# Conditioned transformer block: the second norm's transpose moved from the even to the odd beats, the FFN's first product one beat sooner

## The reference

```
g, b   = t @ gw.T + gb, t @ bw.T + bb                  (one row per batch)
norm(x)= g * x * rsqrt(mean(x*x) + 1e-6) + b
x1     = x + softmax(q k' / sqrt(8)) v Wo              (q, k, v of norm1(x), 16 heads of width 8)
y      = (silu(norm2(x1) @ gate.T) * (norm2(x1) @ hid.T)) @ out.T     (hidden width 512)
result = x + (x1 + y)
```

## Time and profile before

| | |
|---|---|
| median of 3 runs | 251.71 us (250.55 to 251.79) |
| the profiled execution's own time | 252.26 us |
| its span | 250.4 us, so 1.86 us lie around it |
| mean granted TensorE clock | 0.993 of full speed |
| TensorE busy | 230.9 us |
| VectorE busy | 194.0 us |
| ScalarE busy | 156.7 us |
| GpSimd busy | 97.3 us |

### The profile page before, as it was taken

The page is one execution under the profiler, slowest core; times in us unless marked ns, Lnnn a source line. Parts: engine busy times, 40 slices in busy tenths (PEclk is TensorE's granted clock), DMA queues, the critical chain, the costliest instruction groups (busy, mean ns, idle before and its releaser), DMA issues.

```text
span 250.4 us, 8250 instructions
## 1 busy us (share of the span) xinstructions
PE 230.9 (92%) x3116; PEld 191.6 (77%) x3116; DVE 194.0 (77%) x473; ACT 156.7 (63%) x336; POOL 97.3 (39%) x169
## 2 busy tenths in 40 slices
PE   3579899899999999999999999999999999899894
PEld 2478676677778787878888787878787878687894
DVE  4648956668988998889888988898888888654673
ACT  5486565668766876687667766665566556656430
POOL 8654962454252625244524323242323232323320
PEclk9999889999999999999999999999999999999999
DMA  5872424001500060006000430034000000000001
GB/s 163 355 258 99 157 101 166 3 4 62 195 5 24 19 240 26 3 22 251 28 8 21 159 122 7 21 112 148 27 21 5 3 27 21 5 3 21 25 22 42
DMA packets 11203, 18.79 MB, mean 75 GB/s; under 512 B 1468, under 2 KB 4220, under 8 KB 11036
## 3 DMA queue, kind: packets, MB, share of 16 engines
q1 hardware_dynamic: 10780, 17.67, 19.5%
q10 hardware_dynamic: 384, 0.59, 0.7%
HBM read 3.22 MB, written 2.10 MB: 21 GB/s over the span
## 4 chain that ended last, share of the span: by engine, by line
PE 62%; issue 17%; DVE 8%; POOL 7%; ACT 3%; DMA 2%; SPq 0%; POOLq 0%; DVEq 0%; ACTq 0%
PE pv L500 10%; PE score L431 10%; PE proj L564 7%; PE aux L341 5%; PE aux L343 4%; PE aux L342 4%; DVE nmax L822 3%; PE aux L517 2%; PE aux L521 2%; DMA qs<-qp 2%; PE aux L572 2%; POOL inv L983 2%; PE proj L341 2%; PE pv L529 1%; PE aux L512 1%
## 5 line engine op out<-in xcount | busy, mean ns | idle before, releaser
L682 ACT ACTIVATE p_s<-score 128x1024 f32<-128x1024 f32 x64 | 65.7, 1026 | 34.0 <-PE score L431 33.9
L822 DVE TENSOR_REDUCE nmax<-raw 128x8 f32<-128x1024 f32 x60 | 73.1, 1219 | 5.0 <-PE score L413 2.7
L431 PEld LDWEIGHTS score<-qs,ks 32*128 32x128 f32 x512 | 34.1, 186 | 15.0 <-issue 11.5
L431 PE MATMUL score<-qs,ks 32*128 32x128 f32 x512 | 42.8, 284 | 2.7 <-DVE shift L832 1.9
L500 PE MATMUL pv<-p_s,va 128*32 128x128 f32 x1024 | 41.7, 281 | 0.2 <-ACT xn L700 0.2
L413 PE MATMUL raw<-ks,qs 31*128 31x128 f32 x480 | 40.2, 285 | 1.6 <-DMA qs<-qp 1.6
L881 DVE SCALAR_TENSOR_TENSOR gated<-th,aux 128x256 f32<-128x256 f32 x56 | 23.3, 416 | 18.7 <-ACT th L711 18.3
L341 PE MATMUL aux<-xn_hi,ffn_hi 128*128 128x256 f32 x112 | 36.5, 326 | 0.0
L996 POOL TENSOR_TENSOR xn_lo<-xn,xn_hi 128x128 fp32r<-128x128 f32 x32 | 14.7, 460 | 55.6 <-DVE xn_hi L872 55.6
L413 PEld LDWEIGHTS raw<-ks,qs 31*128 31x128 f32 x480 | 31.7, 186 | 1.8 <-DMA qs<-qp 1.8
L564 PE MATMUL proj<-ffn_out_s,hT 128*128 128x128 f32 x240 | 31.6, 275 | 0.0
(11 more groups left out here) (128 smaller groups left out, 431.6 us busy)
## 6 DMA issues: line engine op xcount, KB each, us to landing
ks<-kp SPq DMA_DIRECT2D x23, 256.0 KB, 2.7
qs<-qp SPq DMA_DIRECT2D x23, 256.0 KB, 2.6
out_y<-x_s SPq DMA_DIRECT2D x16, 128.0 KB, 1.8
x_s<-in_x SPq DMA_DIRECT2D x1, 1536.0 KB, 10.4
x_s<-in_x SPq DMA_DIRECT2D x2, 256.0 KB, 3.9
ffn_in_s<-in_ffn_in_w SPq DMA_DIRECT2D x1, 512.0 KB, 6.5
qs<-shift SPq DMA_DIRECT2D x30, 8.0 KB
attn_w_s<-in_attn_w SPq DMA_DIRECT2D x1, 256.0 KB, 5.7
```

The source lines that it names most:

```text
L431: return pe.matmul(score[:, pair_cols(e, j)], ks[buf(g)][tile_rows(e, t, TROWS), j, batch_cols(t)], qs[buf(g)][tile_rows(e, t, TROWS), j, ...
L682: act.activation(p_s[:, n % PBUF, :], score[:], ACT.Exp, scale=SCALE).then_inc(s_exp, 1)
L822: dve.tensor_reduce(heads[:, t % 2, :, :], raw_dst(g, t)[:].rearrange("l (e j m) -> l e j m", e=HALVES, j=HQ), AX.X, ALU.max, negate=True) ...
```

## The change

The four table numbers INV2, XT2, HI2 and FFN each become one smaller. With XT2 = 5 the transpose `d_xt2` falls in the odd beats, where `a_transpose` is, and it is issued directly behind that one and ahead of `d_out` and `c_wo`. HI2 = 6 puts `d_hi` and `d_lo` in the even beats, INV2 = 4 puts `d_inv` and `d_scale` there. FFN = 9 starts the FFN one beat sooner, so beat 9 loses its four unread products. `a_transpose` no longer waits for the second norm's activation of the beat before, and `d_xt2` no longer waits for the copy `c_ot` of the same beat. OUT, FINAL and RESID stay.

```diff
-    OT, TR2, NORM, TRO, WO, X1, INV2, XT2, HI2, RESID = 2, 2, 2, 3, 3, 4, 5, 6, 7, 6
-    FFN, OUT, FINAL, WSTEP = 10, 15, 17, HC + 1
+    OT, TR2, NORM, TRO, WO, X1, INV2, XT2, HI2, RESID = 2, 2, 2, 3, 3, 4, 4, 5, 6, 6
+    FFN, OUT, FINAL, WSTEP = 9, 15, 17, HC + 1
...
                 if T is not None:
                     if T == 1:
                         pe.wait_ge(s_shift0, MB)
-                    for f, i in due(T - 1, XT2, NB, 2):
-                        pe.wait_ge(s_xn2, NB * f + i + 1)
...
-            def d_xt2(g, i, T):
+            def d_xt2(g, i):
                 pe.wait_ge(s_xs2, NB * g + i + 1)
                 if g == G - 1 and i > 0:
                     pe.wait_ge(s_xn2, NB * g + i)
-                for f, n in due(T, OT, NB, 2):
-                    pe.wait_ge(s_ot, NB * f + n + 1)
                 pe.transpose(pv[:, 2 * L:3 * L], xs2[:, i, :], ident[:]).then_inc(s_xt2, 1)
...
                 for g, b in due(T, XT1, NB, 2, since=3):
                     a_transpose(g, b, T)
+                for g, i in due(T, XT2, NB, 2):
+                    d_xt2(g, i)
                 for w in range(WIN):
                     for g, half in due(T, OUT + WSTEP * w, 2):
                         d_out(g, w, half)
                 for g, i in due(T, WO, NB, 2):
                     c_wo(g, i)
-                for g, i in due(T, XT2, NB, 2):
-                    d_xt2(g, i, T)
```

## The result

The changed kernel took 256.44 us, the median of 4 runs (256.31 to 256.79). The kernel before, run beside it, took 251.75 us (4 runs, 250.55 to 253.17). The ratio is 1.0156, with a 95% interval of 1.0117 to 1.0196: slower, by 4.7 us. The forecast was 255.6 us. The profiled execution took 256.79 us with a span of 255.0.

What follows compares the result with a forecast made beforehand. TensorE was taken to bound most beats, VectorE's reduction start beats 2 and 6. Terms 2.9 + 0.9 + 0.5 - 0.5 + 0.1 = +3.9 us gave 255.6 us from the 251.71 median; range 251.4 to 257.4, likeliest case 254.5 to 256.8.

Steps and rivals of the forecast that it cites:

- What bounds: VectorE's start of reduction L822 sets the end of beats 2 and 6; TensorE's own work sets the other six.
- The held copy, 0.72 us four times: Beats 18, 26, 34, 42: moved d_hi copy waits for GpSimd's second subtraction, delaying the maxima 0.72 us each, 2.9 us.
- Not held: Rival: in beat 2 the copy gets in ahead of GpSimd's second subtraction; +0.9, 252.6 us; chance 0.19.
- Sharing: Rival: copy and GpSimd's subtraction both run at about half speed, 0.34 us a time; +2.0, 253.7 us; chance 0.10.
- Held twice: Rival: GpSimd's `d_inv` also gets in ahead of the copy, 5 x 0.62 more; 258.7 us; chance 0.07.
- the bound of 1.34: Upper bound in us per held copy in beat 2, if GpSimd's `d_inv` gets in ahead of it too.
- Faster, by the waits for `c_ot`: Rival: maxima have slack, so TensorE's 2.8 us of waits before transposes and 0.5 at the end go; 248.4 us; chance 0.10.
- Beat 6 and its like, 7 x 0.13 = 0.9: Beats 14, 22, 30, 38, 46, 54, 58: the copy delays the reduction by its issue distance, 0.13 us each.
- The low bound: Lower bound of the beat-6 term: 0.05 a beat as TensorE's slack hides part; sum 0.6 us.
- Beat 10, +0.5: Sooner FFN piece in beat 9 makes beat 10's maxima 0.8 us later, less 0.35 for removed waits; bounds -0.4 and +1.1.
- The end, -0.5: Last batch's norm: GpSimd does `inv` before `resid`, so `xs2` comes 0.5 us earlier; bounds -0.8 and 0.

Runs made afterwards that it cites:

- the early `a_hi`: Changed kernel with VectorE issuing the first norm's two copies (a_hi) ahead of the FFN's hidden product in beat 1; 251.03 us, ratio 0.9913.
- The reduction with one input: Kernel before plus one unread VectorE row-maximum reduction of x1 (128x128, SBUF) per batch, behind the squares' sum; 257.77 us, ratio 1.0234.
- The copy behind the maxima: Changed kernel with d_hi moved between the row maxima (b_max) and the shift (b_shift); 250.86 us, ratio 0.9958.
- the FFN a beat later: Changed kernel with FFN = 10 again, so that only the second norm's steps are moved; 256.96 us, ratio 1.0202.
- The added copies of that kernel: Kernel before plus one unread VectorE copy of x1 to a spare 128x128 tile per batch, behind the squares' sum; 263.54 us, ratio 1.0428.
- the kernel with the copy behind `c_norm`: Changed kernel with d_hi issued behind c_norm, no longer ahead of the row maxima, in all its beats; 258.35 us, ratio 1.0207.

## Why the prediction was right, step by step

- **What bounds.** Right: in the beats 2 and 6 VectorE's start of the reduction sets the end. When it moved by 0.67 the half grew by 0.66, when it moved by 0.13 the half grew by 0.14, and where the early `a_hi` took 1.08 away, 1.06 came back.
- **The held copy, 0.72 us four times.** The mechanism was right, the size a little too large: 0.67 us a time and 2.63 in all. The copy ended 0.08 us behind the subtraction, not 0.15 as in the pair of rows it was taken from, which was of a 128x256 copy (0.15 in all kernels; every held 128x128 copy ended 0.08 to 0.09 behind). The order on the two engines was right too: the squares' sum, held 0.23 us, gets in between the two subtractions, and the copy waits for the second. The Trainium skill's page "SBUF — State Buffer", section "SBUF: two separate sides", describes this as an exclusive lock on the port pair rather than a split of bandwidth, taken by two-port copies and by operations with two SBUF inputs. For GpSimd's subtraction and for `resid` all runs agree with it: beside one of them with 0.66 us left the copy takes 0.74 to 0.76 us, with 0.2 us left 0.28, and with none 0.21 to 0.23. The squares' sum with its two inputs takes 0.29 alone, and 0.31 to 0.58 beside a subtraction with 0.16 to 0.43 left, always ending 0.15 behind it. The reduction with one input takes 0.27 to 0.28 in all 32. For the power `inv` the traces differ from the page, and they decide: it didn't hold the copy. Where one came up in the kernel before with 0.39 us of `inv` left, it took its usual time:

```profile
237.59 0.22 DVE L872 CAST xn_hi<-xn 128x128 fp32r<-128x128 f32 x1
```

- **Not held** fell with the 0.74 us. **Sharing** fell with the length of the copy (0.43 us by half speed, 0.74 measured), with its end just behind GpSimd's instruction (0.08 to 0.09 us in two kernels), and with the reduction that was never slowed. **Held twice** fell: `inv` started at 112.31 and ran 0.54 us, but the copy was over at 112.43, with one hold. By the row just shown `inv` wouldn't have cost the 0.62 us of this rival even ahead of the copy; that price, and with it the bound of 1.34, took a hold by `inv` for granted.
- **Faster, by the waits for `c_ot`** fell as argued. These waits left, and the maxima's wait grew to 0.32 in beat 6. The copy behind the maxima, which removes the cost of the copy and keeps the waits' removal, left the period at 26.60.
- **Beat 6 and its like, 7 x 0.13 = 0.9.** Against the kernel before, four of the seven grew by 0.11 to 0.15 (beats 22, 30, 38, 46), as did 58; beats 14 and 54 didn't (-0.08, -0.02), nor did beat 50 (-0.03). So the sum was +0.56. Against the kernel with the copy behind the maxima, all seven are 0.12 to 0.16 longer, 0.98 in sum, so the copy's price was right. What the sum put at nothing is what left with the transposes and their waits: 0.23 us in beat 14 and 0.14 in beat 54 (that kernel against the kernel before), next to nothing in the steady beats. The low bound, written as 0.05 a beat and summed to 0.6, is 0.08 a beat (0.13 less 0.05).
- **Beat 10, +0.5** came out at +0.50, with the copy held there as well (the wait at L473 1.21 us). It was more than luck: with the FFN a beat later the stretch is 0.41 us shorter than before (the forecast credited 0.35 for the waits that left), and the sooner FFN, with the hold of the copy that comes with it, puts 0.91 on it (forecast 0.8).
- **The end, -0.5.** Only -0.17. This term was mis-sized, though its reason was right: `inv` does come first, and from the last addition of `x1` to the transpose it took 1.77 us (241.26 to 243.03) instead of 2.25 (236.26 to 238.51). But that addition itself came 0.23 later behind the last maxima's transpose, and the rest of the run was 0.08 longer. The rows of the end, against the earlier trace rows:

```profile
241.96 0.54 POOL L979 TENSOR_TENSOR inv<-ms,mhalf 128x1 f32<-128x1 f32 x1 [4.16 <-DVE ms L860]
...
243.03 0.33 PE L525 MATMUL pv<-ident,xs 128*128 128x128 f32 x1 [1.27 <-POOL xs L985]
```

- **What the sum left out.** The clock at the start: 1.08 us of the span's growth, and about as much of the medians' difference. By its steps the forecast was +3.9; the change is worth +2.9 to +3.3 at equal clock, and +3.5 by the table without its first row, so the steps are 0.4 to 1.0 too high. The medians are 4.7 apart because the runs of the changed kernel stood one level of the clock below those of the kernel before. That 255.6 came within 0.9 us of 256.44 is thus in part luck: the steps' excess and the clock's share that they left out have opposite signs.

Still open: why the granted clock differs between executions, why the power `inv` doesn't hold the copy, and whether ScalarE could write the second norm's rounded part (not tried).

## What to carry to other kernels

Before a copy or an operation with two SBUF inputs is moved on VectorE, look at what GpSimd runs at the new place: a copy of 0.22 us cost 0.67 beside a subtraction there, as part of a chain that TensorE waits for. Put it where VectorE waits anyway, but not behind its consumer's need: one place later than that cost 0.20 us a piece and 2 us at the end. And where a kernel's executions differ by a level of the clock, compare at equal clock before any story about 1 us is told.

## What was unexpected of the hardware

- The addition of `resid` (0.83 us on GpSimd) held the copy as the subtraction did: 0.75 us in both. The added copies of that kernel took 0.22 to 0.23 us in the beats 0 and 4 and 0.74 to 0.76 in the beats 2 and 6, none between.
- The power `inv` on GpSimd held no copy: 0.22 us for the copy with 0.39 us of it left. The hold can also go the other way: in the kernel with the copy behind `c_norm`, the copy at 241.15 came up 0.01 us behind the start of `xs2`'s scaling, took its 0.22, and the scaling took 0.49 us instead of 0.40.
- A `tensor_reduce` of one SBUF tile was held in none of 32 cases, beside the same subtraction that held the squares' sum of 0.29 us to 0.52.
- The granted clock of the first 40 us differs between executions of one kernel. The changed kernel took 253.8, 255.0 and 256.4 us at mean clocks of 1.000, 0.993 and 0.986, and the kernel before 250.5, 251.7 (252.1 in one series) and 253.1.
